# Mixture of experts: tagged rows and a scatter back to token order, in place of gathers

## The reference, cut to what matters

```
x      = rmsnorm(src + attention @ Wo, norm1_w)
shared = swiglu(x @ W_shared_in) @ W_shared_out          # 256 -> 512 -> 256
hidden = swiglu(x @ W1_shared)                           # 512 wide, the same for all experts
group, expert logits -> softmax; 8 experts, the best 2 of the best group, weights p1 and p2
y      = p1 * hidden @ W2[e1] + p2 * hidden @ W2[e2]     # W2[e]: 512 x 256
out    = x5 + rmsnorm(x + shared + y, norm2_w)
```

## Time and profile before

| what | value |
|---|---|
| median of three runs | 5847.61 us |
| the profiled execution's own time | 5839.69 us |
| its span | 5837.6 us |
| busy share of the span: PE, DVE, ACT, POOL | 86%, 67%, 54%, 42% |
| mixture-of-experts stage | from about 5175 us to the end |
| of it: step loop, slot loop, what follows the last slot | 5175 to 5574.7, 5574.7 to 5773.5, 5773.5 to 5837.6 |

### The profile page before, as it was taken

One profiled execution on the slowest core, in us unless ns is written; L12 is line 12 of the kernel. 1 busy time (PEld: TensorE's weight loads), 2 busy tenths in 40 slices (PEclk: granted clock), 3 DMA queues, 4 the chain that ended last, 5 costly groups with the idle time before them and its releaser, 6 DMA issues. The chain is left out here.

```text
span 5837.6 us, 139849 instructions
## 1 busy us (share of the span) xinstructions
PE 5046.7 (86%) x53868; PEld 3302.1 (57%) x53868; DVE 3899.9 (67%) x6903; ACT 3133.8 (54%) x4732; POOL 2458.5 (42%) x2096
## 2 busy tenths in 40 slices
PE   7688888888798889788889989997889999989994
PEld 3455555555487544377778778885532333346674
DVE  5899999999796955544444434444689888844424
ACT  5899999999654845422222223333445666642221
POOL 1778787788565623343444432112530000001114
PEclk9899999999999999889999989998798999999997
DMA  5202020020111133422323321112652222232256
GB/s 169 50 17 53 14 49 21 26 36 13 39 45 51 54 132 154 163 95 99 105 101 107 107 96 63 46 51 54 164 147 43 45 46 46 44 97 68 77 161 188
DMA packets 441106, 457.16 MB, mean 78 GB/s; under 512 B 227874, under 2 KB 376728, under 8 KB 432272
## 3 DMA queue, kind: packets, MB, share of 16 engines
q1 hardware_dynamic: 418704, 397.99, 24.1%
q0 software_dynamic: 8192, 25.17, 1.3%
q10 hardware_dynamic: 13568, 25.17, 1.2%
HBM read 276.38 MB, written 171.82 MB: 77 GB/s over the span
## 5 line engine op out<-in xcount | busy, mean ns | idle before, releaser
L538 POOL TENSOR_SCALAR attn_u<-attn_rel,attn_aux 128x1024 f32<-128x1024 f32 x512 | 1088.5, 2126 | 267.6 <-DVE attn_nm L565 267.5
L689 PE MATMUL attn_tp<-attn_ident,attn_pr 128*128 128x128 f32 x4096 | 571.0, 283 | 242.8 <-ACT attn_pt L628 240.8
L3366 DVE TENSOR_REDUCE attn_mx<-attn_mp 128x1 f32<-128x512 f32 x1024 | 652.6, 685 | 91.7 <-PE attn_mp L3445 90.7
L689 PEld LDWEIGHTS attn_tp<-attn_ident,attn_pr 128*128 128x128 f32 x4096 | 446.7, 143 | 463.2 <-ACT attn_pt L628 325.7
L557 DVE SCALAR_TENSOR_TENSOR attn_u<-attn_rel,attn_aux,attn_u 128x1024 f32<-128x1024 f32 x512 | 681.6, 1331 | 26.6 <-POOL attn_u L538 18.0
L3430 ACT ACTIVATE attn_pt<-attn_st 128x1024 f32<-128x1024 f32 x512 | 506.5, 1022 | 283.3 <-PE attn_st L3456 282.7
L649 ACT ACTIVATE attn_pr<-attn_pr,attn_nm 128x1024 f32<-128x1024 f32 x512 | 603.6, 1179 | 85.4 <-DVE attn_nm L565 85.3
L565 DVE CUSTOM_DVE_ANT_0 attn_pr<-attn_u,attn_s 128x1024 f32<-128x1024 f32 x512 | 619.5, 1210 | 42.0 <-PE attn_s L680 30.5
L628 ACT ACTIVATE attn_pt<-attn_tp 128x512 f32<-128x512 f32 x1024 | 566.6, 623 | 8.1 <-issue 5.2
L3445 PE MATMUL attn_mp<-attn_kt,attn_qt 96*128 96x512 bf16 x1024 | 371.9, 394 | 17.6 <-DMA attn_qt<-s_q 16.6
L680 PE MATMUL attn_s<-attn_kt,attn_qt 96*128 96x512 bf16 x1024 | 315.5, 391 | 50.6 <-DMA attn_kt<-s_k 23.8
(11 more groups left out here) (549 smaller groups left out, 10720.0 us busy)
## 6 DMA issues: line engine op xcount, KB each, us to landing
s_qkv<-gin_qkv SPq DMA_DIRECT2D x32, 1536.0 KB, 5.0
core_qk<-s_qkv SPq DMA_DIRECT2D x32, 1024.0 KB, 5.0
attn_qt<-s_q SPq DMA_DIRECT2D x384, 64.0 KB, 3.0
attn_kt<-s_k SPq DMA_DIRECT2D x192, 128.0 KB, 4.2
moe_rows<-s_hid_s SPq DMA_DIRECT2D x78, 256.0 KB, 2.8
core_arow<-s_alr SPq DMA_DIRECT2D x32, 512.0 KB
core_grow<-s_gar SPq DMA_DIRECT2D x32, 512.0 KB, 3.6
core_vv<-s_qkv SPq DMA_DIRECT2D x32, 512.0 KB, 3.5
```

The lines of the kernel that those rows point to most:

```text
L538: pool.tensor_scalar(u[:, x % 4], rel[:, z % 2, 1], aux[:, s, 4 + NH + h:5 + NH + h], aux[:, s, 4 + 2 * NH + h:5 + 2 * NH + h], ALU.mult, ...
L689: ins = pe.transpose(tp[k][:, n], pr[:, x % BUF, (4 * k + n) * P:(4 * k + n + 1) * P], ident[:])
L3366: dve.reduce_max(mx[w % 2][:].rearrange("p h t a -> p (h t a)")[:, j:j + 1], bank(("row", number))[:], AX.X).then_inc(m["max_done"], 1)
```

## The change

The result rows are no longer gathered by POOL. Every hidden row gets a **tag** of two values: its row in a token-ordered result buffer `y_t` (token number, plus T for the second choice), and its weight. POOL scatters the 8-byte tags beside the hidden rows into `tag_s`. SP loads a slot's tags with its rows. DVE's `copy_out` multiplies by the weight and turns the first value into an index, and POOL scatters the slot's results by it into `y_t` (`results`). The results then come back by plain loads from SP (`load_results`), two for a pair, and DVE adds them with two wide additions. Pad rows get spare tags that point behind the 2T rows. Unused slots now read blocks of their own: seven zero blocks for each half are written at the start, and `tables` needs neither the minimum nor the last six instructions (for `gidx`). `pad(1)` is spread, one expert in each of slots 2 to 9. Two loads from SP ahead of the loop of zero writes are new, with a wait for them.

```diff
-            def pad(h):
+            def pad(h, experts):
                 sp.wait_ge(m["table_done"], h + 1)
-                for n in range(NE):
+                for n in experts:
                     row = sp.value_load(pads[0:1, h, n:n + 1], min_val=0, max_val=2 * SORTED - P)
                     sp.dma_start(d["hid_s"][bass.ds(row, P), :], zero[:]).then_inc(m["pad_out"], 16)
+                    sp.dma_start(d["tag_s"][bass.ds(row, P), :], spare[:, h, n]).then_inc(m["pad_out"], 16)
...
                 sp.dma_start(rows[:, s % 4], d["hid_s"][bass.ds(row, P), :]).then_inc(e["row_in"][s % 4], 16)
-            def store_rows(s):
-                h, at_ = s // SL, s % SL * P
-                sp.wait_ge(m["y_copy"], s + 1)
-                sp.dma_start(d[f"y_s{h}"][at_:at_ + P, :], yb[:, s % 3]).then_inc(e["y_out"][s % 3], 16)
+                need(sp, "y_copy", s - 3)
+                sp.dma_start(tags[:, s % 4], d["tag_s"][bass.ds(row, P), :]).then_inc(e["row_in"][s % 4], 16)
+
+            def load_results(c):
+                h = c // HALF
+                if c % HALF == 0:
+                    for n in range(3):
+                        sp.wait_ge(e["y_out"][n], 16 * (h + 1) * SL // 3)
+                need(sp, "acc2", c - 3)
+                for k in range(TOPK):
+                    at_ = k * T + c * 2 * P
+                    sp.dma_start(g[:, c % 4, k], d["y_t"][at_:at_ + 2 * P, :].rearrange("(z p) c -> p z c", p=P)).then_inc(e["g_in"][c % 4], 16)
...
+            sp.dma_start(tag[:], d["moe_tag"]).then_inc(m["tag_in"], 16)
+            sp.dma_start(spare[:], d["moe_spare"]).then_inc(m["tag_in"], 16)
+            sp.wait_ge(m["tag_in"], 32)
+            sp.wait_ge(m["consts"], 1)
             for h in range(2):
-                sp.wait_ge(m["consts"], 1)
-                sp.dma_start(d["hid_s"][h * SORTED + ZERO_ROWS:h * SORTED + ZERO_ROWS + P, :], zero[:]).then_inc(m["zero_out"], 16)
+                at_ = h * SORTED + ZERO_ROWS
+                sp.dma_start(d["hid_s"][at_:at_ + 7 * P, :].rearrange("(n p) c -> p n c", p=P),
+                             zero[:].rearrange("p (o c) -> p o c", o=1).to_broadcast([P, 7, HID])).then_inc(m["zero_out"], 16)
+                sp.dma_start(d["tag_s"][at_:at_ + 7 * P, :].rearrange("(n p) c -> p n c", p=P), spare[:, h, NE:]).then_inc(m["zero_out"], 16)
...
             for s in range(LAST):
-                if s == 2:
-                    pad(1)
+                if 2 <= s < 2 + NE:
+                    pad(1, (s - 2,))
                 if s + 3 < LAST:
                     load_rows(s + 3)
-                if s >= 1:
-                    store_rows(s - 1)
                 if tail(s) and tail(s)[1] == 0:
+                    load_results(tail(s)[0])
                     load_x5(tail(s)[0])
-            store_rows(LAST - 1)
+            for c in range(HALF, HALF + 2):
+                load_x5(c)
             for c in range(HALF, PAIRS):
-                load_x5(c)
+                load_results(c)
+                if c >= HALF + 2:
+                    load_x5(c)
@@ POOL
                     for k in range(TOPK):
                         pool.indirect_dma_start(d["hid_s"], bass.IndirectOffsetOnAxis(idx[:, t, k:k + 1], 0), hid[:, t % 4], None
                                                 ).then_inc(e["sc_out"][t % 4], 16)
+                        pool.indirect_dma_start(d["tag_s"], bass.IndirectOffsetOnAxis(idx[:, t, k:k + 1], 0), tag[:, t, k], None
+                                                ).then_inc(e["tag_out"][t % 2], 16)
+            def results(s):
+                pool.wait_ge(m["home_done"], s + 1)
+                pool.wait_ge(m["y_copy"], s + 1)
+                pool.indirect_dma_start(d["y_t"], bass.IndirectOffsetOnAxis(home[:, s % 3], 0), yb[:, s % 3], None).then_inc(e["y_out"][s % 3], 16)
...
-            for h in range(2):
-                ...
-                for c in range(h * HALF, h * HALF + HALF):
-                    gather(c)
+            for s in range(LAST):
+                results(s)
+                if tail(s) and tail(s)[1] == 2:
+                    last_root(tail(s)[0])
+            for c in range(HALF, PAIRS):
+                last_root(c)
@@ DVE
             def copy_out(s):
-                dve.wait_ge(m["ob_mm"], s + 1)
+                dve.wait_ge(e["row_in"][s % 4], 32 * (s // 4) + 32)
                 if s >= 3:
                     dve.wait_ge(e["y_out"][s % 3], 16 * (s // 3))
-                dve.tensor_copy(yb[:, s % 3], ub[s % 2][:, 0:D]).then_inc(m["y_copy"], 1)
+                dve.tensor_copy(home[:, s % 3], tags[:, s % 4, 0:1]).then_inc(m["home_done"], 1)
+                dve.wait_ge(m["ob_mm"], s + 1)
+                dve.tensor_scalar(yb[:, s % 3], ub[s % 2][:, 0:D], tags[:, s % 4, 1:2], None, ALU.mult).then_inc(m["y_copy"], 1)
...
+                dve.wait_ge(e["g_in"][c % 4], 32 * (c // 4) + 32)
+                both = acc[:, 2 * c:2 * c + 2]
+                dve.tensor_tensor(both, both, g[:, c % 4, 0], ALU.add).then_inc(m["acc1"], 1)
+                dve.wait_ge(m["acc1"], c + 1)
+                dve.tensor_tensor(both, both, g[:, c % 4, 1], ALU.add).then_inc(m["acc2"], 1)
@@ PE
             def turn_rows(s):
-                pe.wait_ge(e["row_in"][s % 4], 16 * (s // 4) + 16)
+                pe.wait_ge(e["row_in"][s % 4], 32 * (s // 4) + 32)
```

More of the change, by code:

```diff
@@ L3551, in stage_moe @@
         pick, posn, posf = r.sb("pick", [P, 2, TOPK, NE]), r.sb("posn", [P, 2, NE]), r.sb("posf", [P, TILES, TOPK])
-        fe, shift, moved = r.sb("fe", [P, NE]), r.sb("shift", [P, HT * TOPK, NE]), r.sb("moved", [P, HT * TOPK])
-        idx, gidx = [r.sb(n, [P, TILES, TOPK], mybir.dt.uint32) for n in ("idx", "gidx")]
-        wsel = r.sb("wsel", [P, TILES, TOPK])
+        idx = r.sb("idx", [P, TILES, TOPK], mybir.dt.uint32)
+        tag, spare, tags = r.sb("tag", [P, TILES, TOPK, 2]), r.sb("spare", [P, 2, NE + 7, 2]), r.sb("tags", [P, 4, 2])
+        home = r.sb("home", [P, 3, 1], mybir.dt.uint32)
         cnt, num, cumi = r.sb("cnt", [P, NE]), r.sb("num", [P, NE]), r.sb("cumi", [P, NE])
@@ L3569, in stage_moe @@
                  "at_mm at_c wo_mm xs_done sq_done var_done rs_done x_done xt_mm xt_c l_mm dif_done ex_done m_done pf_mm pos_done "
-                 "u_mm sil_done mul_done so_mm acc0 cn_mm cnt_done table_done gidx_done pad_out zero_out chain "
+                 "tag_in u_mm sil_done mul_done so_mm acc0 cn_mm cnt_done table_done pad_out zero_out home_done chain "
                  "tb_mm rt_c ob_mm y_copy acc1 acc2 sq2_done var2_done rs2_done yn_done out_done")
         m = {n: r.sem(n) for n in names.split()}
-        e = {n: [r.sem(f"{n}{k}") for k in range(c)] for n, c in (("a_in", 2), ("sc_out", 4), ("row_in", 4), ("y_out", 3), ("g_in", 4),
+        e = {n: [r.sem(f"{n}{k}") for k in range(c)] for n, c in (("a_in", 2), ("sc_out", 4), ("tag_out", 2), ("row_in", 4), ("y_out", 3), ("g_in", 4),
                                                                  ("x5_in", 2), ("out", 2))}
@@ L3618, in load_rows @@
                         sp.wait_ge(e["sc_out"][n], 32 * HT * (h + 1) // 4)
-                    sp.wait_ge(m["pad_out"], 16 * NE * (h + 1))
+                    for n in range(2):
+                        sp.wait_ge(e["tag_out"][n], 32 * HT * (h + 1) // 2)
+                    sp.wait_ge(m["pad_out"], 32 * NE * (h + 1))
                     if h == 0:
-                        sp.wait_ge(m["zero_out"], 32)
+                        sp.wait_ge(m["zero_out"], 64)
                 need(sp, "tb_mm", s - 3)
@@ L3662, in _ @@
                 if i == HALF + 1:
-                    pad(0)
+                    pad(0, range(NE))
             for s in range(3):
@@ L3700, in scatter @@
                                                 ).then_inc(e["sc_out"][t % 4], 16)
-            def gather(c):
-                for z in range(2):
-                    t = 2 * c + z
-                    need(pool, "acc2", t - 3)
-                    for k in range(TOPK):
-                        pool.indirect_dma_start(g[:, t % 4, k], None, d[f"y_s{c // HALF}"], bass.IndirectOffsetOnAxis(gidx[:, t, k:k + 1], 0)
-                                                ).then_inc(e["g_in"][t % 4], 16)
+                        pool.indirect_dma_start(d["tag_s"], bass.IndirectOffsetOnAxis(idx[:, t, k:k + 1], 0), tag[:, t, k], None
[4 more added lines that the diff above has]
+                pool.indirect_dma_start(d["y_t"], bass.IndirectOffsetOnAxis(home[:, s % 3], 0), yb[:, s % 3], None).then_inc(e["y_out"][s % 3], 16)
             def last_root(c):
@@ L3719, in _ @@
                     scatter(i)
-            for h in range(2):
-                for n in range(3):
-                    pool.wait_ge(e["y_out"][n], 16 * (h + 1) * SL // 3)
-                pool.wait_ge(m["gidx_done"], h + 1)
-                for c in range(h * HALF, h * HALF + HALF):
-                    gather(c)
-                    if c > h * HALF:
-                        last_root(c - 1)
```

(15 more changed lines are left out.)

23 lines of the change are left out of this document (3 added, 20 removed).

## The result

The changed kernel is slower: 5856.2 us (median of 20 runs, 5844.4 to 5871.6) against 5835.8 (20 runs, 5824.7 to 5856.9) in the same company, a ratio of 1.0035 with an interval of 1.0026 to 1.0044. Forecast was 5834 us. The time lies inside the range given, but the sign was wrong: 20 us slower, not 11 faster. The difference is a third of a percent, and clear of no change. The profiled execution has a span of 5850.5 us against 5837.6.

The account below looks back on a forecast made before the run. It took PE to bound the step loop and slots, and POOL's gathers the stretch after the last slot. Terms -12.2 + 7.1 - 3.0 + 19.2 gave 11.1 us gained, from 5845 to 5834 us, range 5815 to 5858.

Parts of the forecast that it names:

- 1, stage start: Start of the stage: writes and a wait put ahead of the third pair's inputs lose 12.2 us, ends 2 and 23.
- zeros 7.8: Stage start: 14 zero blocks in place of 2, 3.15 MB more at 401 GB/s, take 7.8 us.
- cover 7.9: Stage start: third pair's last input landed 7.9 us before PE took it, so that much delay is free.
- the spare tags: Stage start: 1792 spare tags of 8 bytes, 112 packets per engine at 27 ns, cost 3.0 us.
- the wait for the tag loads: Stage start: SP goes on 5.5 us later, part of it hidden; 3.9 us taken, ends 0 and 5.5.
- The clock term: Stage start: after its standstill PE's next slot runs slower, 2.4 us more.
- 2, step loop: Step loop after the start: four tag scatters per pair on POOL and more pads on SP are hidden; zero, ends 0 and 2.
- 3, first slots: First slots: half 1's pads laid out over slots at SP's 3.05 us each; gain 7.1 us, ends 2.7 and 13.1.
- 4, the other slots: Later slots: tags land in time, zero; beside half 0's results late loads lose 3.0 us, ends -1.6 and 12.
- results come late: Rival, beside half 0's results: the later slots' waits reach 12 us; 2 us gained, 5843 us; chance 0.17.
- 5, after the last slot: After the last slot: plain loads replace POOL's gathers, 3.9 us a pair; gain 19.2 us, ends 11 and 22.5.
- Tags jam the queue: Rival, stage start: tiny tag writes at 0.25 us a packet take 28 us; 14 us slower, 5859 us; chance 0.16.

Follow-up runs that it names:

- b1: Kernel before with only half 1's pads laid out, one expert in each of slots 2 to 9, no tags; ratio 0.9994 to the kernel before.
- e3: Changed kernel with eight tag buffers in place of four; slots 204.5 us against 217.3, ratio 1.0024 to the kernel before.
- c4: Changed kernel with zero rows and spare tags after third pair's inputs, eight tag buffers, results one pair ahead, pads at slots 6, 10, ... 34; ratio 0.9966 to before.
- e5: Changed kernel with result loads issued one pair ahead; after the last slot 42.5 us against 48.0, slots 220.1 us.
- c7: c4 with six buffers of slot results in place of three; median 5814.6 us, ratio 0.9956 to the kernel before.
- c1: Changed kernel with zero rows and spare tags after third pair's inputs, eight tag buffers, results one pair ahead, pads at slots 2, 6, ... 30; ratio 0.9962 to before.
- e4: Changed kernel with half 1's pads and their tags at slots 2, 6, ... 30 instead of 2 to 9; slots 235.7 us against 217.3.

## Why the prediction was wrong, step by step

- **1, stage start** (12.2 lost, ends 2 and 23): 16.0 measured. The mechanism, the place and the two largest terms hold: zeros 7.8 and cover 7.9 leave 0.56 us, with POOL's scatters (without tags) in the same trace. Too small were the spare tags (3.0, ends 1.9 and 9.2; measured 4.9, to about 1 us) and the wait for the tag loads, of which I let the engines' backlog hide a part (3.9; 4.2 us of SP idle, none of it hidden, and some 5 more in the landing, which I had at 3.0 for POOL). The clock term was 2.4; 16.0 less the stall of 14.9 leaves 1.1.
- **2, step loop** (0): right. POOL's idle before the root shrank from 11.67 us to 8.53, and nothing behind it moved. The row after (POOL):

```profile
5265.94 0.72 POOL L3709 TENSOR_TENSOR moe_rs<-moe_va,moe_half 128x2 f32<-128x2 f32 x1 [8.53 <-DVE moe_va L3772]
```

- **3, first slots** (7.1 gained; 4.0 lost): the first half of what failed. "With a pad and its tags 3.05" us of SP for a slot was 3.73, and "land some 2.2 us later" was 5.2 for slot 5 and up to 7.0 behind the next pads. From slot 0's turn the tags of slot 5 go out after 9.9 us (forecast 8.7), it is turned after 15.1 (10.9), and the next seven slots take 27.9 (21.4). So SP's pace is worth some 5 us of the 11 that this term is off, and the landing the 3.0 of slot 5 and its further growth. Both lie outside the ends that were given (3.5 us a slot, landing 3.5).
- **4, the other slots** (3.0 lost; 14.4 lost): the second half. The sentence was "the tags have from 0.6 us after slot s-1's matmuls to the end of slot s+1's, some 3.7 us, for a landing of 2.2 to 2.6". The 3.7 us were right (3.6 measured), and for most plain slots so was the landing, though it was taken from a 26 KB load in another stage. What was wrong is to take an ordinary landing for the latest one. About every eighth slot of the plain ones has 3.9 to 4.2 us: 0.4 us too late, and 1.3 us longer for PE (5.3 in four). Beside results three landed after 4.8 to 5.1 us. "Zero" for the plain slots should have been a price for the slots that come late, since the next slot doesn't win back what one loses.
- The account of the 18.4 us over both: pads laid out -6.7 (b1); late tags +12.8 (e3 against after), nearly all of it from slot 13 on; 10.79 us a pair beside results for 10.55, +1.9 over eight pairs, which I put down to two more instructions and a dearer copy on DVE (not tried alone); the rest, 204.5 - 192.2 - 1.9 = 10.4, is pads with tags in slots 2 to 9 (45.0 us to slot 13 in e3, 34.7 in b1) and goes when they stand from slot 6 at every fourth (c4: 193.6).
- The rival *results come late* had a part of the right place and the wrong cause (e5): beside the slots DVE waits 2.4 us in all for `moe_g`. Late tags, which it names only as traffic, were the cause.
- **5, after the last slot** (19.2 gained): 16.1. The 3.9 us a pair are as forecast, and the first additions came 6.6 us after the last copy (forecast 7.2). What was off is "the stores behind are the same": from DVE's end (5842.26) to the end of the span are 8.2 us, and 5.6 before (5832.03 to 5837.6). c7, e3 and e5 have 8.1 to 8.3 there too; why is open.
- *Tags jam the queue*: 0.25 us a packet was far off, 0.044 measured; yet the sign of this rival came true by the sum of smaller things, to which I had given no case. Its 5859 us lies close to the measured 5856.2 by luck: it gives a loss of 14 us where 20 were measured, on a base of 5845 us, from four times, that the 20 runs put 9 us lower.

Why does a load of 1 KB take over 2 us at all? In the plain slots of after the tags go out 1.06 us behind the 256 KB of their rows and landed 2.4 us after that (median). Where they went out 1.9 to 2.8 us behind the rows they landed after 1.7 us in four slots of five (2.2 in the fifth). In c1's trace they go out 0.5 us behind and took 2.4 us at the least, 3.6 in the median and 4.7 at most, beside 3.4 in the median for the rows. The view of the tile `tags` in c1:

```profile
DMA to landing us min/median/max: 2.4/3.6/4.7
```

The Trainium skill (DMA: Bandwidth & Descriptors, section Queues, rings and completion order) says that the increment of a semaphore lands only after all earlier writes of the same DMA engine. The rows agree: a small load lands just behind the large one before it. That rule also fits the four stalls, where one engine was behind. By itself it wouldn't have turned the forecast: with the rows' median landing of 2.8 us in the trace of before step 4 still has 0.9 us of slack. Their longest landing there was 6.0.

## What to carry to other kernels

A small load that stands behind a large one lands just after it: price it with the landing of what is issued just ahead of it, and with the writes beside it. Where a load waits for the same event that its user is two steps behind, ask for the latest landing and not the ordinary one: with a slack of 1.2 us over the ordinary landing, four late loads in 32 cost 5.3 us. Another set of buffers for a few bytes was worth 12.8 us here. Where the issuing engine sets the pace, as in the first slots, more buffers bring nothing, and spreading its work does (c4). And count what is put ahead of an input that has cover: 7.8 us of zeros were free, and the next 14 us were not.

## What was not expected of the hardware

- Writes of 8 bytes cost what is behind them some 44 ns a packet and DMA engine (112 packets, 4.9 us, from two traces). The packets themselves were taken up in 1.2 us, and in 2 us behind them the DMA engines moved 48 GB/s.
- One 16 KB packet of instructions in one DMA engine stood beside each of the eight late landings of tags in the plain slots of two traces (3.7 to 4.3 us in place of 2.4), with 15 of 16 engines done in time.
- SP needs 0.54 us from one DMA issue to the next there. From the end of an issue to the next one with an address read between it takes 0.9 to 1.05 us (5595.50 to 5596.40, 5597.29 to 5598.34), not the 0.75 of the earlier trace rows.
- Thinning out pads made the slots 18 us longer (e4), and with eight tag buffers it made them 4 shorter (c1 against e3).
- The same kernel had step loops of 409.8 and 398.9 us in two executions (c4), most of it in PE's wait for the prefix sum.
